# Span words read once a pair of groups, and one `Silu` ahead of ScalarE's loop, in the attention stage of a graph network

## The reference

```python
def _mlp(x, w0, b0, w1, b1):
    return jax.nn.silu(x @ w0 + b0) @ w1 + b1
...
w_ij = _mlp(edge_feats, rad_w0, rad_b0, rad_w1, rad_b1)
w_ij = w_ij + _mlp(chi_scalar, sph_w0, sph_b0, sph_w1, sph_b1)
w_ij = w_ij.reshape(-1, H, HD)
q = (node_feats @ wq).reshape(-1, H, HD)[receivers]
k = (node_feats @ wk).reshape(-1, H, HD)[senders]
alpha = (q * w_ij * k).sum(axis=-1) / jnp.sqrt(jnp.float32(HD))
alpha = alpha * cutoffs[:, None]
v = (node_feats @ wv).reshape(-1, H, HD)[senders]
out = jax.ops.segment_sum(alpha[..., None] * v, receivers, num_segments=n_nodes) / AVG_NUM_NEIGHBORS
```

## Time and profile before

| what | before |
|---|---|
| median of 3 runs | 9111.23 us (9110.14 to 9121.32) |
| the profiled execution, own time | 9110.68 us |
| its span | 9108.8 us |
| mean granted TensorE clock | 0.91 of full speed |
| TensorE, share of the span busy | 83% |
| VectorE | 66% |
| ScalarE | 57% |
| GpSimd | 38% |
| attention stage, from the first gather to the end of the last gather's issue | 6198.7 to 9057.2 us |

### The profile page before, as it was taken

The page is one execution under the profiler, slowest core; times in us unless marked ns, Lnnn a source line. Parts: engine busy times, 40 slices in busy tenths (PEclk is TensorE's granted clock), DMA queues, the critical chain, the costliest instruction groups (busy, mean ns, idle before and its releaser), DMA issues. The chain is left out here.

```text
span 9108.8 us, 195691 instructions
## 1 busy us (share of the span) xinstructions
PE 7570.4 (83%) x51013; PEld 5736.6 (63%) x51014; DVE 6053.3 (66%) x12579; ACT 5236.3 (57%) x9302; POOL 3425.6 (38%) x4082
## 2 busy tenths in 40 slices
PE   5999999888869998989998877887777777777775
PEld 3655666577769996666666555555565556555654
DVE  7888998899964446555555555556566656666656
ACT  3666666688757775444444433345556656666653
POOL 0000000000000002666666666655555556566655
PEclk8999999999989998999999888778889888898886
DMA  3333333466646661222222211114555555555554
GB/s 113 138 135 135 137 138 136 153 225 225 213 141 183 183 183 60 63 63 63 63 63 63 55 45 45 45 43 151 159 161 166 161 156 165 166 162 162 165 160 128
DMA packets 511184, 1177.41 MB, mean 129 GB/s; under 512 B 98171, under 2 KB 171308, under 8 KB 491685
## 3 DMA queue, kind: packets, MB, share of 16 engines
q1 hardware_dynamic: 381834, 858.67, 28.9%
q0 software_dynamic: 129280, 317.93, 12.5%
HBM read 899.64 MB, written 276.57 MB: 129 GB/s over the span
## 5 line engine op out<-in xcount | busy, mean ns | idle before, releaser
L2271 POOL DMA_INDIRECT att_kv_rows<-kv_dram,att_stage x1616 | 1632.7, 1010 | 629.7 <-issue 439.2
L2011 POOL DMA_INDIRECT conv_rows<-y_dram,conv_stage x1616 | 1563.3, 967 | 642.2 <-issue 557.3
L695 PE MATMUL conv_part<-conv_msgs,conv_hot 128*128 128x256 f32 x3232 | 939.7, 443 | 0.0
L842 PE MATMUL att_mlp<-mlp_feats,mlp_w 64*128 64x512 f32 x1568 | 522.5, 742 | 435.6 <-ACT mlp_hid L862 429.0
L2034 PEld LDWEIGHTS conv_w_ps<-conv_w,conv_hid 100*128 100x128 f32 x3248 | 466.0, 221 | 656.8 <-issue 314.2
L1967 ACT ACTIVATE conv_hid<-conv_hid_ps 100x512 f32<-100x512 f32 x408 | 243.5, 597 | 1093.7 <-PE conv_hid_ps L2029 701.5
L2086 DVE TENSOR_TENSOR conv_t<-conv_rows,conv_harm 128x384 f32<-128x384 f32 x404 | 226.1, 560 | 953.8 <-DMA conv_rows<-y_dram,conv_stage 947.2
L2034 PE MATMUL conv_w_ps<-conv_w,conv_hid 100*128 100x128 f32 x3248 | 553.6, 322 | 308.1 <-DVE conv_msgs L2100 228.1
L851 PE MATMUL att_mlp<-mlp_w,mlp_hid 128*128 128x128 f32 x6272 | 790.8, 288 | 19.2 <-issue 18.8
L851 PEld LDWEIGHTS att_mlp<-mlp_w,mlp_hid 128*128 128x128 f32 x6272 | 773.1, 204 | 35.7 <-issue 35.2
L695 PEld LDWEIGHTS conv_part<-conv_msgs,conv_hot 128*128 128x128 f32 x3232 | 701.4, 228 | 105.2
(11 more groups left out here) (278 smaller groups left out, 15928.7 us busy)
## 6 DMA issues: line engine op xcount, KB each, us to landing
c_dram<-count_counts SPq DMA_DIRECT2D x392, 392.0 KB, 2.4
mean_counts<-c_dram SPq DMA_DIRECT2D x343, 448.0 KB, 3.4
w_dram<-mlp_w SPq DMA_DIRECT2D x404, 256.0 KB
att_w_rows<-w_dram SPq DMA_DIRECT2D x404, 256.0 KB
soft_counts<-c_dram SPq DMA_DIRECT2D x98, 1024.0 KB, 4.9
mlp_feats<-in_feats SPq DMA_DIRECT2D x405, 192.0 KB
soft_counts<-c_dram SPq DMA_DIRECT2D x49, 1088.0 KB, 5.0
att_lanes<-lo_dram SPq DMA_DIRECT2D x404, 128.0 KB
```

Source lines behind the costliest of these rows:

```text
L695: ins = nc.tensor.matmul(part, c.hot[:, s, t, :], rows[:, t, :], start=half == 0 and t == 0, stop=half == 1 and t == T - 1)
L842: nc.tensor.matmul(self.hid_ps[:, n], self.w0[rows, m * P:(m + 1) * P], self.feats[rows, :], start=True, stop=True).then_inc(self.hid_sum, 1)
L2011: pool.indirect_dma_start(rows[:, s, t, :], None, y_dram, bass.IndirectOffsetOnAxis(ap=stage[:, s, t:t + 1], axis=0)).then_inc((gathered[s ...
L2271: pool.indirect_dma_start(kv_rows[:, s, t, :], None, kv_dram, bass.IndirectOffsetOnAxis(ap=stage[:, s, t:t + 1], axis=0)).then_inc((gather ...
```

## The change

A `Reach` is made once a pair of groups by VectorE for its groups' `q_of_turns` and, for the first pair of an iteration, its `add`, and by TensorE in the same way for `pick_q_x` and `turns`. It is made at the beginning of group 0 and group 2, so ahead of the waits of these groups, and its registers are kept until they have been used. `q_windows` keeps its own reads, and so does what is done in group 1 for the last pair of the iteration before. Ahead of ScalarE's loops in the attention stage stands one `Silu` of one column; it writes into `mlp.hid`, which nothing reads at that point. In `conv_edges` the `Reach` is made by the caller at the place where it was made before.

```diff
-def lane_sums_x(nc, pe, c, s, k, rows):
-    reach = Reach(pe, c.spans, k)
+def lane_sums_x(nc, pe, c, s, reach, rows):
...
                 copy_q(1, 1)
+
+                nc.scalar.activation(mlp.hid[:, 0, 0:1], mlp.b0[:, 0:1], ACT.Silu)
                 with act.Fori(0, twos) as i:
...
-                def pick_q_x(k, s):
-                    reach = Reach(pe, spans, k)
+                def pick_q_x(reach, s):
...
                 def body(i, first, per, last=False):
                     for s in range(S):
                         g, k = S * i + s, 2 * i + s // 2
+                        if s == 0:
+                            early = Reach(pe, spans, k)
+                        elif s == 2:
+                            late = Reach(pe, spans, k)
                         if s < 2 or not last:
...
-                        pick_q_x(k, s)
+                        pick_q_x(early if s < 2 else late, s)
...
                         if s == 3:
-                            turns(i, 1)
+                            turns(1, early)
                         elif s == 1 and not first:
-                            turns(i - 1, S - 1)
+                            turns(S - 1, Reach(pe, spans, k - 1))
...
                 def body(i, first, last, per):
                     own = Steps(dve, own_done, i * (4 * S))
                     for s in range(S):
                         g, k = S * i + s, 2 * i + s // 2
+                        if s == 0:
+                            early = Reach(dve, spans, k)
+                        elif s == 2:
+                            late = Reach(dve, spans, k)
                         if s % 2 == 1 and not last:
...
-                        q_of_turns(Reach(dve, spans, k), k, s, g)
+                        q_of_turns(early if s < 2 else late, k, s, g)
...
                         if s == 1 and not first:
-                            add(i - 1, S - 1)
+                            add(i - 1, S - 1, Reach(dve, spans, k - 1))
                         if s == 3:
-                            add(i, 1)
+                            add(i, 1, early)
```

More of the change, by code:

```diff
@@ L2044, in turns @@
                 def turns(i, s):
-                    lane_sums_x(nc, pe, c, s, 2 * i + s // 2, lambda t: msgs[:, s - 1 + t // T, t % T])
+                    lane_sums_x(nc, pe, c, s, Reach(pe, spans, 2 * i + s // 2), lambda t: msgs[:, s - 1 + t // T, t % T])
                 def body(i, early, unit):
@@ L2297, in sums, with turns @@
                     lane_sums(nc, pe, c, s, g, k, msgs[:, s])
-                def turns(i, s):
-                    lane_sums_x(nc, pe, c, s, 2 * i + s // 2, lambda t: msgs[:, s - 1 + t // T, t % T])
-                def pick_q_x(k, s):
-                    reach = Reach(pe, spans, k)
+                def turns(s, reach):
+                    lane_sums_x(nc, pe, c, s, reach, lambda t: msgs[:, s - 1 + t // T, t % T])
+                def pick_q_x(reach, s):
                     with pe.If(reach.more() > 0):
@@ L2352, in _ @@
                 sums(NI - 1, S - 1)
-                turns(NI - 1, S - 1)
+                turns(S - 1, Reach(pe, spans, 2 * NI - 1))
             @block.vector
@@ L2402, in q_of_turns, with add @@
                             own.do(nc.vector.tensor_tensor(q, q, in_halves(here), ALU.add))
-                def add(i, s):
-                    k = 2 * i + s // 2
-                    lane_add(nc, dve, c, s, S * i + s, k, Reach(dve, spans, k))
+                def add(i, s, reach):
+                    lane_add(nc, dve, c, s, S * i + s, 2 * i + s // 2, reach)
                 def body(i, first, last, per):
@@ L2453, in _ @@
                 body(NI - 1, False, True, 0)
-                add(NI - 1, S - 1)
+                add(NI - 1, S - 1, Reach(dve, spans, 2 * NI - 1))
 def laid_out(inputs):
```

## The result

The change makes the kernel slower: 9162.6 us in the median of 4 runs (9154.4 to 9169.8) against 9110.7 of 4 runs of the kernel before beside them, a ratio of 1.0057 [1.0039, 1.0074]. The forecast was 9082, in a range from 9045 to 9135. The profiled execution takes 9163.7 us, its span is 9161.9. One execution of a later kernel (the eleven with TensorE's pick behind its sums) took 20965 us at a clock of 0.44, and the ratio of that kernel leaves it out.

The account below looks back on a forecast made before the run. GpSimd's own gather loop was taken to bound the attention stage. From 9110.7 us: 0 for table loads, -48 for the earlier burst, +20 taken back, -0.4 for the tail, giving 9082, range 9045 to 9135.

Parts of the forecast that it names:

- VectorE's 0.4 us: Attention stage: without the read, VectorE's product with q comes 0.4 us earlier in every group; no time by itself.
- the forecast's own sign: Attention stage: the forecast is wrong if GpSimd's period doesn't fall below 28.1 us with all else in place.
- the term for the earlier burst: SyncE's loads for the next iteration, issued together, come 0.4 us earlier: 48 us gained, 20 us taken back.
- the near class: The 66 iterations whose burst begins within 6.8 us of group 3's gathers; mean 27.81 us; all iterations should become like them.
- the split of the earlier trace: Attention iterations divided by burst distance from group 3's gathers: 66 within 6.8 us take 27.81 us, 25 later take 29.37.
- the 48 us: Attention stage: gain if all iterations become like the 66, 28.3 - 27.81 = 0.49 us by 98.
- The 20 us taken back: Attention stage: 0.2 us an iteration lost as the earlier store and loads meet group 3's last landings and group 0's.
- Slower: Rival, 9146 us: the earlier burst meets group 3's or the next group's third gather, 1.56 us per long iteration; chance 0.14.
- Nothing moves: Rival, 9110 us: the burst's 1.5 MB must pass beside some gather, and where it begins may not matter; chance 0.26.
- ScalarE on the path: Rival, 8985 to 8860 us: the attention loop's removed table loads save 126 us, or 251 with both; chance 0.05.
- the loads stay: Rival: 196 table loads remain in the attention loop; time that of the reads alone, 9082 us; chance 0.05.

Follow-up runs that it names:

- the eleven with TensorE's pick behind its sums: Changed kernel with VectorE's product reading q in PSUM and TensorE's pick for two groups ahead moved to the end of a group's step: 9204.9 us, 1.0005.
- the two gap kernels: Changed kernel with an unused span-word read behind VectorE's first product, in every group: 9134.5 us, 1.0024; in group 2 alone: 9112.8 us, 1.0010.
- the short gap: Changed kernel with four increments of a semaphore nobody waits for, behind VectorE's first product of group 2 alone: 9139.3 us, 1.0024.
- the burst put back: Changed kernel with one unused span-word read on SyncE ahead of an iteration's second store, so its burst of loads comes later: 9175.6 us, 1.0077.
- the last pair: SyncE's loads issued one group at a time instead of in a burst, on the kernel before: 9044.4 us, 0.9923; on the changed kernel: 9013.2 us, 0.9886.

## Why the prediction was wrong

*Right:* that GpSimd's own loop is the bound; that the 196 table loads go, and that they and TensorE's reads are covered (the time moved by ratios of 1.0010 and 1.0001); the counts; VectorE's 0.4 us in every group (idle time 197.6 to 15.0 us); the burst at 6.3 us behind group 3's gathers.

*The step that failed* is "VectorE's 0.4 us is no time by itself, as its wait for the next gather only grows". It took VectorE as something that reaches GpSimd by a wait or through SyncE's burst alone. It reaches it by a third way that no row of waits shows: a gather that begins while VectorE is in an operation with two inputs in SBUF (`qk`, the product with q, the messages, 0.69 us each) lasts until 0.8 us behind that operation's end. The read had kept the product off group 3's second gather. The iteration, which by the forecast's own sign had to fall below 28.1 us, rose to 28.83. Term missing from the sum: 0.66 us an iteration, times 98, +65 us; with the 18 us that the tail of group 0 did give, 9110.7 + 65 - 18 = 9158 of the 9163.7 measured. Shown by the product with an input in PSUM (no hold in the same place), by the two gap kernels (group 3's hold gone once its product is moved) and by the edge of the short gap.

The Trainium skill says where the two engines meet ("GPSIMD Engine Reference", section "Specifications"): GpSimd shares its SBUF interfaces with VectorE, with contention from VectorE instructions in a two-port mode or with two inputs in SBUF. This trace agrees, with the gather of 1.34 us beside one of 0.95; I hadn't weighed it.

*Mis-sized besides:* the term for the earlier burst, -48 + 20 = -28 us. The tail of group 0 shortened by 0.18 us, 18 us. The burst moved into the near class in practically all iterations, and this tail did become that class's: in the trace before it is 4.68 us in the iterations with the burst within 6.8 us and 5.3 in the later ones, and 4.67 after the change. But the split of the earlier trace rows was read as the price of the burst alone, and it holds two things. Of the 1.56 us between the two classes only 0.64 is the tail. Another 0.66 is group 0's first three gathers, 2.86 us together in the near class and 3.52 in the later one. That is the very hold that the sum lacks, already in the trace before and put down to the burst. A smaller slip is in the 48 us as well: they start from 28.3 us, the stage by its 101 iterations, and not from the split's own mean of 28.24, which would make 42. The 20 us taken back had no row, and no run shows them.

On the chip where the kernel before takes 9198 the tail of group 0 shortened by 1.39 us, 136 us. So the forecast of one number hung on a term that differs eightfold between two chips, against a loss that differs little (0.66 and 0.83 us an iteration).

*The rivals.* "Slower" came true by its sign only; its mechanism, the burst in other gathers, is refuted by the burst put back (1.0077). "Nothing moves" is refuted, "ScalarE on the path" and "the loads stay" too.

*Open:* why group 0's tail is longer on one chip than on another, and whether it is the earlier burst that shortens it there; and the 0.51 us of tails in the last pair.

## What to carry to other kernels

Where one engine's chain of its own bounds a stage, look at how long each of its instructions lasts and not only at what it waits for. Here the same gather took 0.95 us or 1.34, no wait named the cause, and the busy time of the engine as a whole (2.1 us more) hid it. Before an operation of VectorE is moved, lay its new place over GpSimd's gathers in the timeline; a pause on an engine with slack may be what keeps two engines apart. Iterations split by one event show a direction and no price, since something else may differ between the two kinds (here the held gathers), and it takes a kernel with that event alone moved (here the loads taken out of their burst, 0.8%) to learn what it is worth.

## What the runs showed of the hardware

- A gather (0.95 us) that begins 0.045 us or more into a VectorE operation with two inputs in SBUF lasts until 0.81 to 0.86 us behind its end (up to 1.52 us in all). One that is already under way isn't lengthened; then the VectorE operation is, from 0.69 to 0.77 us at most in the rows shown. The product with an input in PSUM holds nothing: 237 gathers begin during it, of 0.96 us at most.
- Two inputs aren't the only such case. The scaling of `cut` (L2447, a TENSOR_SCALAR of 128x1616, one tensor in and out of SBUF, 1.00 us) runs once; a gather that begins during it lasts 1.38 us, until 0.82 us behind its end. This was seen and not tested.
- ScalarE's table stays loaded through the loops of the stage: one `Silu` ahead of the loop took away 196 loads, at 1.28 us each.
- The same kernel before took 9103, 9111, 9114, 9118 and 9198 us in the median on the chips that it ran on, the changed one 9163 and 9155, the latter on the chip of the 9198.
